# Forming the lower parts of q and k on VectorE, straight from the projections in PSUM, in a fused attention and mixture-of-experts kernel

## The reference

```python
def attn(x):                       # H = 8 heads, dk = 16
    xn = layernorm(x) * gamma + beta
    q = (xn @ Wq + bq) by heads;  k = (xn @ Wk + bk) by heads;  v = (xn @ Wv + bv) by heads
    p = softmax(q k^T / sqrt(dk)); att = p v
    return att summed over the groups of 8 that its reshape makes
def ffn(u):                        # E = 8 experts, top 2
    gates = sigmoid(u @ centroids.T), the two largest kept and normalised
    return sum over experts of gate * (gelu(u W1[e] + b1[e]) W2[e] + b2[e])
x = x + attn(layernorm(x))
x = x + ffn(layernorm(x))
```

## Time and profile before

| | |
|---|---|
| median of 3 runs | 707.14 us (706.84 to 707.73) |
| the profiled execution | 707.2 us |
| its span, first to last instruction | 705.4 us |
| mean granted TensorE clock, share of full | 0.937 |
| TensorE products busy | 578.7 us (82%) |
| VectorE busy | 523.7 us (74%) |
| GpSimd busy | 494.2 us (70%) |
| ScalarE busy | 486.6 us (69%) |

### The profile page before, as it was taken

One profiled execution on the slowest core, in us unless ns is written; L12 is line 12 of the kernel. 1 busy time (PEld: TensorE's weight loads), 2 busy tenths in 40 slices (PEclk: granted clock), 3 DMA queues, 4 the chain that ended last, 5 costly groups with the idle time before them and its releaser, 6 DMA issues.

```text
span 705.4 us, 14432 instructions
## 1 busy us (share of the span) xinstructions
PE 578.7 (82%) x3889; PEld 440.5 (62%) x3889; DVE 523.7 (74%) x1557; ACT 486.6 (69%) x904; POOL 494.2 (70%) x571
## 2 busy tenths in 40 slices
PE   3799998988988989869976888689999999999200
PEld 1566766666666666636644666468888888888200
DVE  7578898988898888888852688457777777777274
ACT  3467878787777787755665887478888888888000
POOL 6434557888888888857886567757788788877700
PEclk9999999999999999979995899899999999999755
DMA  4645545554545645444325567998777778786099
GB/s 118 176 97 153 151 123 159 164 157 136 143 138 162 169 131 155 121 119 121 108 64 163 162 207 212 258 247 263 243 221 246 244 217 246 250 252 198 12 389 324
DMA packets 107570, 127.31 MB, mean 180 GB/s; under 512 B 19950, under 2 KB 86010, under 8 KB 106497
## 3 DMA queue, kind: packets, MB, share of 16 engines
q1 hardware_dynamic: 89600, 105.34, 51.4%
q0 software_dynamic: 9088, 16.94, 7.3%
q10 hardware_dynamic: 8832, 4.46, 2.1%
HBM read 69.26 MB, written 33.72 MB: 146 GB/s over the span
## 4 chain that ended last, share of the span: by engine, by line
PE 38%; POOL 20%; issue 9%; DMA 6%; DVE 6%; ACT 4%; SPq 2%; POOLq 0%; ACTq 0%; DVEq 0%
POOL slots L590 9%; PE ps_max L948 4%; PE ps_max L949 4%; PE ps_max L950 4%; DMA probs<-comb 3%; DMA probs<-slots 3%; PE ps_proj L1001 2%; PE ps_route L993 2%; PE ps_st L948 2%; PE ps_st L949 2%; PE ps_st L950 2%; PE ps_av L851 2%; PE ps_st L833 2%; PE ps_max L821 2%; POOL att_n L600 2%
## 5 line engine op out<-in xcount | busy, mean ns | idle before, releaser
L657 POOL DMA_INDIRECT comb<-probs,gate_row x156 | 179.8, 1152 | 42.9 <-issue 38.9
L1032 DVE TENSOR_REDUCE row_max<-ps_max 128x2 f32<-128x512 f32 x256 | 173.9, 688 | 47.4 <-PE ps_max L821 42.9
L682 ACT ACTIVATE probs<-ps_st 128x512 f32<-128x512 f32 x256 | 146.8, 594 | 57.6 <-PE ps_st L833 55.3
L1257 DVE TENSOR_TENSOR k_stack<-probs,k_stack 128x512 fp32r<-128x512 f32 x156 | 108.1, 693 | 75.1 <-ACT k_stack L783 73.0
L590 POOL DMA_INDIRECT slots<-y_row,slot_idx x128 | 125.5, 980 | 39.2 <-issue 37.6
L821 PE MATMUL ps_max<-k_stack,q_stack 96*128 96x256 f32 x512 | 132.6, 344 | 24.0 <-DVE row_max L1032 22.9
L821 PEld LDWEIGHTS ps_max<-k_stack,q_stack 96*128 96x128 f32 x512 | 81.8, 198 | 71.9 <-DVE row_max L1032 47.0
L833 PE MATMUL ps_st<-q_stack,k_stack 128*128 128x256 f32 x512 | 106.6, 291 | 13.2 <-ACT probs L682 12.8
L833 PEld LDWEIGHTS ps_st<-q_stack,k_stack 128*128 128x128 f32 x512 | 79.6, 192 | 21.3 <-ACT probs L682 19.1
L851 PE MATMUL ps_av<-probs,v_aug 128*32 128x256 f32 x1024 | 70.3, 393 | 0.0
L780 ACT ACTIVATE probs<-ps_st,b_cur 128x512 f32<-128x512 f32 x78 | 53.9, 692 | 23.1 <-DMA b_cur<-b_all 17.5
(11 more groups left out here) (175 smaller groups left out, 1275.2 us busy)
## 6 DMA issues: line engine op xcount, KB each, us to landing
q_stack<-w_split SPq DMA_DIRECT2D x78, 512.0 KB, 4.3
probs<-slots SPq DMA_DIRECT2D x39, 260.0 KB
q_stack<-q_hi SPq DMA_DIRECT2D x64, 128.0 KB, 2.7
k_stack<-k_hi SPq DMA_DIRECT2D x64, 128.0 KB, 3.0
probs<-comb SPq DMA_DIRECT2D x8, 1024.0 KB, 7.8
X<-in_L_attn_x_dram SPq DMA_DIRECT2D x16, 256.0 KB, 3.3
q_stack<-q_lo SPq DMA_DIRECT2D x32, 128.0 KB, 2.7
k_stack<-k_lo SPq DMA_DIRECT2D x32, 128.0 KB, 3.0
```

The source lines that it names most:

```text
L657: pool.indirect_dma_start(comb_rows, bass.IndirectOffsetOnAxis(gate_row[r][:, c, 1:2].bitcast(I32), 0), res[r][:, c * P:(c + 1) * P], None ...
L682: act.activation(probs[slot % 2][:, h, :, :], ps_st[h % 2][:], ACT.Exp, scale=DK ** -0.5).then_inc(exp_done, 1)
L1032: dve.tensor_reduce(row_max[slot % 2][:, sc, 2 * hp:2 * hp + 2], ps_max[k % 2][:], AX.X, ALU.max).then_inc(smax_reduced, 1)
L1257: dve.tensor_tensor(lo, x, hi.bitcast(F32), ALU.subtract).then_inc(s, 1)
```

## The change

`q_f32` and `k_f32` go, with the two ScalarE copies that write them and their waits. GpSimd's `lo_part` goes. VectorE forms (ps_proj + bias) - hi in one instruction: for k in unit 4 of even periods, behind the transposition of att, for q in unit 7 of odd periods, behind the reduction. TensorE now also waits for `q_lo` ahead of the projection of k and for `k_lo` ahead of the transposes of z, since both are read out of `ps_proj`.

```diff
@@ SBUF
-        q_f32 = sb("q_f32", [P, 512])
-        k_f32 = sb("k_f32", [P, 512])
@@ GpSimd
-            def lo_part(n, par, x, hi, lo, hi_ready, lo_ready):
-
-                wait(pool, hi_ready, n + 1)
-                pool.tensor_tensor(lo[par][:], x[:], hi[par][:].bitcast(F32), ALU.subtract).then_inc(lo_ready, 1)
...
-                if not t.odd and t.pair(2):
-                    n, par = t.pair(2)
-                    lo_part(n, par, k_f32, k_hi, k_lo, k_hi_ready, k_lo_ready)
...
-                if t.odd and t.pair(3):
-                    n, par = t.pair(3)
-                    lo_part(n, par, q_f32, q_hi, q_lo, q_hi_ready, q_lo_ready)
@@ ScalarE
                         wait(act, k_proj, n + 1)
-                        wait(act, k_lo_ready, n)
-                        act.activation(k_f32[:], ps_proj[:], ACT.Identity, bias=bk_c[:, 0:1])
                         act.activation(k_hi[par][:], ps_proj[:], ACT.Identity, bias=bk_c[:, 0:1]).then_inc(k_hi_ready, 1)
...
-                        wait(act, q_lo_ready, n)
-                        act.activation(q_f32[:], ps_proj[:], ACT.Identity, bias=bq_c[:, 0:1])
                         act.activation(q_hi[par][:], ps_proj[:], ACT.Identity, bias=bq_c[:, 0:1]).then_inc(q_hi_ready, 1)
@@ TensorE
                         wait(pe, q_hi_ready, n + 1)
+                        wait(pe, q_lo_ready, n + 1)
                         pe.matmul(ps_proj[:], Wk_p[:], xnT[par][:], start=True, stop=True).then_inc(k_proj, 1)
...
                         wait(pe, k_hi_ready, n)
+                        wait(pe, k_lo_ready, n)
                         for c in range(4):
                             last = pe.transpose(ps_proj[:, c * P:(c + 1) * P], z[:, c, :], ident[:])
...
             pe.wait_ge(k_hi_ready, B // 2)
+            pe.wait_ge(k_lo_ready, B // 2)
@@ VectorE
+            def proj_lo(n, par, bias, hi, lo, hi_ready, lo_ready):
+
+                wait(dve, hi_ready, n + 1)
+                dve.scalar_tensor_tensor(out=lo[par][:], in0=ps_proj[:], scalar=bias[:, 0:1], in1=hi[par][:].bitcast(F32),
+                                         op0=ALU.add, op1=ALU.subtract).then_inc(lo_ready, 1)
...
+                prep_q = t.pair(3) if t.odd else None
+                prep_k = None if t.odd else t.pair(2)
...
                         dve.reciprocal(rden[slot % 2][:], att[slot % 2][:, :, :, DK]).then_inc(rden_ready, 1)
+                    if k == 4 and prep_k:
+                        n, par = prep_k
+                        proj_lo(n, par, bk_c, k_hi, k_lo, k_hi_ready, k_lo_ready)
+                    if k == 7 and prep_q:
+                        n, par = prep_q
+                        proj_lo(n, par, bq_c, q_hi, q_lo, q_hi_ready, q_lo_ready)
```

## The result

The changed kernel takes 701.1 us (median of 10 runs, 699.37 to 705.18) against 707.07 us of the kernel before (10 runs, 705.73 to 707.98): a ratio of 0.9913 (0.9898 to 0.9928). The forecast was 701.7 us. The profiled execution took 701.01 us, its span is 699.3 us.

The account below looks back on a forecast made before the run. GpSimd was taken to bound the stretch of ten pairs of batches, not the whole kernel. Ten pairs -6.1, the rest +0.6, sum -5.5 from 707.2: 701.7 us; range 694.0 to 705.5, carried on to 706.5.

Parts of the forecast that it names:

- GpSimd was last, and 2.6 us a pair off it frees the pair: Ten pairs of batches: without two subtractions GpSimd's need falls from 21.34 to 18.8 us a pair, no longer last.
- ScalarE at nothing beyond 0.57: ScalarE in the pairs: copies save 1.1 us a pair, costed at nothing beyond 0.57 in the second chain.
- The added instruction at 0.60 us, start to start: VectorE's new subtraction out of PSUM: 0.60 us each in a full queue, 1.2 us a pair, at most 1.28 each.
- q_lo 0.45: Behind an odd period's last reduction: TensorE's product for unit 2 stands 0.45 us a pair (between 0 and 0.6).
- k_lo 0.6 in full: Even unit 4, ahead of the reduction TensorE's unit 7 waits for: 0.6 us a pair (between 0 and 0.6).
- Collisions 0.1: VectorE operations on two SBUF tiles stretched beside GpSimd: 0 to 0.5 us a pair, taken as 0.1.
- Ten pairs -6.1: Stretch 95.55 to 306.69 us: ten pairs take 205.0 for 211.1 us, 20.5 a pair.
- +0.6 in front, 0 behind: Before 95.55 us: +0.3 in the fill, +0.3 for batches with VectorE nearly full; behind 306.69 us: 0.
- Rival (a): Collisions go and the handover swallows both additions: pairs of 19.33 us, about 690 us; chance 0.07, below 694.
- Rival (b): Collisions stay at 0.5, q_lo isn't absorbed: pair 21.0, about 707 us, VectorE last, nothing won; chance 0.08.
- Rival (c): VectorE stands in unit 4 for k_hi, delaying reduction and rden: pair 21.7, about 714 us, slower; chance 0.10.
- The range: Forecast 0.75 from 694.0 (pair of 19.7) to 705.5 us (pair of 20.9), carried on to 706.5.

Follow-up runs that it names:

- e9: Changed kernel with GpSimd's two subtractions a pair put back into tiles nobody reads: 712.6 us against 710.71 of the kernel before, ratio 1.0014.
- e10: Kernel before with only q_lo formed by VectorE, k_lo left on GpSimd with its ScalarE copy: 707.16 us against 710.71, ratio 0.9949.
- e1: Changed kernel with ScalarE's two full-precision copies put back unread, on a slower chip: 766.33 us against 775.18 of the kernel before, ratio 0.994, inconclusive.
- e11: Changed kernel with k_lo moved from even unit 4 to behind odd unit 0's reduction: 698.04 us, ratio 0.9816 to the kernel before.
- e8: The changed kernel itself, run again beside the repeated experiments on the same chip: 704.3 us, ratio 0.9896 to the kernel before.

## Why the prediction was right, point by point

- **GpSimd was last, and 2.6 us a pair off it frees the pair.** Right; e9 puts 2.1 of them back and the gain is gone. GpSimd's own need (18.8 us) was far enough below 20.5 for the crossing ring not to matter in the changed kernel, where VectorE never waits for GpSimd between 93.9 and 299 us. In e10 it did matter.
- **ScalarE at nothing beyond 0.57.** Its busy time fell by 10.6 us in the ten pairs, and by itself that brings nothing (e9). That it adds nothing beside a relieved GpSimd wasn't resolved (e1).
- **The added instruction at 0.60 us, start to start.** 0.63 to 0.66 while batches are in flight, with a duration of 0.71 to 0.75 where I had expected 0.66 to 0.72. The upper bound of 1.28 was far off.
- **q_lo 0.45.** The walk's own figures give 96.83 - 96.40 = 0.43. TensorE stood 0.30 us where I looked. Like for like, in the first pair, 0.55 comes through (19.88 in e10 less 19.33): VectorE's gap of 0.53 us, which was to take up its 0.60, still measures 0.46. In a quiet later pair it would be 19.7 (e11) less 19.33, 0.37, but no run shows that 19.33 is what such a pair takes without q_lo.
- **k_lo 0.6 in full.** Right: 0.6 by e11 and 0.65 by the first pair. It was the most expensive step of the change, and one that could be avoided; the prediction saw the place and didn't ask for a better one.
- **Collisions 0.1.** Too low. The excess of the ten pairs over 20.3 us adds up to 2.2 us, 0.22 a pair. I had the mechanism but took rstd for what would hit VectorE next; it was the weight split, 1.0 to 1.4 us once a pair, which held a VectorE instruction up in pairs 2, 3, 7 and 10, and att_n in pair 7. e8 and the profiled run after differ in it (20.32 and 20.82 for pair 7): small shifts decide.
- **Ten pairs -6.1.** Measured -7.05. The pair itself, 20.5, came out right (20.49), and that close it was luck: in the first pair the two additions cost 1.20 us (20.53 less 19.33) for 1.05, the collisions 0.22 for 0.1, and against both a quiet later pair is 0.2 us shorter than the first (20.3 for 20.53), which the prediction didn't have. Of the 0.95 between -6.1 and -7.05, 0.8 is the cut: the ten pairs of the kernel before are 211.14 us in the earlier trace rows and 211.94 by the cut that both kernels have.
- **+0.6 in front, 0 behind.** Wrong in parts. The first reduction comes 0.7 us later (24.81 for 24.10), but by 93.9 us this is made good. TensorE, the bound as I took it, is busy 63.73 us of that stretch instead of 66.21, and GpSimd 20.79 instead of 34.17: there was slack that my reading of the 94% had ruled out. Which wait it came from I did not trace. Behind the pairs the tail gained 1.5 us. The expert half, which forms no q or k and which I had at 0, lost 2.5. Its first load of split weights is issued 8.5 us earlier (360.04 for 368.58), but TensorE's queue stands at the last transposes of routed rows, which ScalarE has to scale first, and ScalarE waits for the landing of the last scatters. After, then before:

```profile
366.98 1.65 ACT L698 ACTIVATE y_row<-X,shift,rstd 128x128 f32<-128x128 f32 x4 [6.83 <-DMA slots<-y_row,slot_idx]
...
368.69 1.12 PE L901 MATMUL ps_route<-ident,y_row 128*128 128x128 f32 x4 [7.25 <-ACT y_row L698]
```

```profile
372.47 1.65 ACT L711 ACTIVATE y_row<-X,shift,rstd 128x128 f32<-128x128 f32 x4 [6.07 <-DMA slots<-y_row,slot_idx]
...
374.17 1.12 PE L916 MATMUL ps_route<-ident,y_row 128*128 128x128 f32 x4 [5.44 <-ACT y_row L711]
```

  Of the 8.6 us by which the stretch begins earlier, 7.3 are left when TensorE comes to this wait, 5.5 when it leaves it, and 7.2 at the first transposes of the expert layer (369.60 for 376.76, where TensorE stood another 1.5 us for a load). So 1.4 of the 2.5 us are gone by then, nearly all of them ahead of the wait, and 1.1 go later. Those 1.1 can't be told from none: from its first transposes to the end the expert layer takes 328.6 us in the profile of the kernel before and 329.7 to 332.8 in the six others of the undisturbed chips, with the same instructions. Where the 1.3 ahead of the wait go is open; no run was made for it.
- **Rival (a)** had the collisions gone and k_lo absorbed. As the kernel stands, neither happened. **Rival (b)** would have a pair of 21.0. The Trainium skill ("Perfetto Trace Analysis", Optimizing Scalar/DVE Operations) has it that GpSimd and VectorE share a read port, so that moving work between them might not help. The trace agrees that they collide, at 0.22 us a pair; moving the work helped all the same: 2.6 us a pair off GpSimd brought 0.7.
- **Rival (c)**, the wait for k_hi: VectorE waited for k_hi once, in the fill, 1.48 us. With GpSimd no longer late ScalarE isn't either. The argument against (c) held.
- **The range.** By the pairs named, 19.7 and 20.9, its inner bounds are 693.7 and 705.7 rather than 694.0 and 705.5; nothing hangs on the difference.
- **The sum**, -5.5 forecast, -6.2 measured between the profiled executions (707.2 and 701.01 us): the pair was right to 0.01 us, by errors that cancel, and the 0.7 us between the two sums lie in the cut and in the edges, where +0.3, +0.3, 0 and 0 stand against a measured 0 in front, -1.5 in the tail and +2.5 in the expert half.

## What to carry to other kernels

When a full engine is relieved, the gain is set by the place at which the work lands on the next engine: walk to the instruction behind each candidate place and ask who waits for that one. A place where the engine stands for another costs nothing (k_lo in unit 4 cost 0.6 us a quiet pair, behind unit 0 none that showed: 6 us of the whole). And compare not each engine's own need with the period, but also the rings that cross engines, since work taken off one of them may still lie in such a ring.

## What was not expected of the hardware

- A VectorE instruction on two SBUF tiles can stand until the GpSimd instruction that runs beside it has ended, however small it is itself: in the changed kernel `gate_sum`, 128x4, 0.16 us alone, took 1.28 and `picked` 0.17 and 0.62, in the kernel before `den` 0.17 and up to 0.73. It need not: `picked` at 117.26 us of the changed kernel lies wholly beside the split that holds `gate_sum` up right after it, and takes 0.17. The new instruction, with one input in PSUM and one in SBUF, was never stretched: the 32 took 709 to 751 ns, and 13 of the 16 for q_lo ran beside a computing instruction of GpSimd. GpSimd's lengths vary too (the weight split 1.03 to 1.37 us, att_n 0.62 to 0.80); with what, I did not trace.
- With two operations (add a bias, subtract) and a PSUM input, the new instruction takes 0.71 to 0.75 us, little more than the 685 ns of the plain subtraction in the earlier trace rows. With pairs in flight the next one starts 0.08 to 0.09 us before it ends.
- The same program took 9% more time on two of the chips than on the others, with short stalls of several engines at once. The mean granted TensorE clock was 0.90 to 0.93 there, against 0.92 to 0.95 on the others. Most of it falls into the expert layer, 373 to 389 us there for 329 to 333. What stalls the engines stays open.
